# A decoder layer with routed experts on one core: token rows scattered to the experts, results scattered back by token

## What is computed

```python
x = _layernorm(x + _L0_attn_ref(x, ...))      # a mamba block: in-projection, conv, selective scan, out-projection
x = _layernorm(x + _L0_xattn_ref(x, ctx, ctx, ...))  # attention to the context, layer norms, FFN 256 -> 1024 -> 256
x = _layernorm(x + _L0_ffn_ref(x, ...))       # the experts, below
# experts: a router gives each token 8 of 160 experts, with gates that sum to 2.5
#   routed = sum over the token's 8 experts of  gate * (silu(x @ w_gate[e].T) @ w_down[e].T)   (256 -> 128 -> 256)
#   shared = silu(x @ w_gate_shared.T) @ w_down_shared.T
#   result = routed + shared
```

## Time and profile before

| | |
|---|---|
| runs | 1699.87 us median (1698.13 to 1703.37) |
| the profiled execution's own time | 1708.86 us |
| its span | 1707.1 us |
| PE, DVE, ACT, POOL busy | 1000.4, 1122.7, 580.4, 880.6 us |
| DVE in 40 slices (tenths) | 1898989999999899999998423344434322224444 |
| POOL in 40 slices | 1545355555655565466374643554544445455664 |
| DMA in 40 slices | 7322140500501401302300000577767787633332 |
| TensorE's granted clock, mean | 0.795 of full speed |

### The profile page before, as it was taken

How to read it: one execution, slowest core, us unless ns; L and a number is a source line. 1 busy time by engine, 2 the same in 40 slices (tenths; PEclk the granted TensorE clock), 3 DMA queues, 4 the chain that set the end, 5 groups by cost and what they waited for, 6 DMA issues and landing times. The chain is left out here.

```text
span 1707.1 us, 20590 instructions
## 1 busy us (share of the span) xinstructions
PE 1000.4 (59%) x4460; PEld 801.9 (47%) x4460; DVE 1122.7 (66%) x2190; ACT 580.4 (34%) x1476; POOL 880.6 (52%) x751
## 2 busy tenths in 40 slices
PE   4567778586676676676577650477767676710000
PEld 2445567474565565564465540466656555500000
DVE  1898989999999899999998423344434322224444
ACT  3564647346335345344342110133332333300000
POOL 1545355555655565466374643554544445455664
PEclk8788789698798788787888775698889899955555
DMA  7322140500501401302300000577767787633332
GB/s 237 128 72 102 44 142 15 183 1 20 179 2 49 149 13 51 135 13 62 117 13 19 13 6 7 160 204 215 209 197 218 195 240 213 188 120 102 106 115 80
DMA packets 118558, 185.00 MB, mean 108 GB/s; under 512 B 16225, under 2 KB 82529, under 8 KB 118114
## 3 DMA queue, kind: packets, MB, share of 16 engines
q1 hardware_dynamic: 97426, 137.72, 24.4%
q0 software_dynamic: 21072, 46.64, 11.2%
HBM read 152.26 MB, written 57.22 MB: 123 GB/s over the span
## 5 line engine op out<-in xcount | busy, mean ns | idle before, releaser
L413 POOL TENSOR_TENSOR inf<-bc,du 128x1024 f32<-128x1024 f32 x128 | 302.0, 2365 | 194.0 <-DVE DA L974 85.0
L743 PE MATMUL Y<-hb,ident 128*128 128x256 f32 x1024 | 280.2, 423 | 60.7 <-DVE hb L981 37.4
L1335 POOL DMA_INDIRECT xg<-x_dram,idb x216 | 205.6, 952 | 207.3 <-DVE idb L1493 94.3
L974 DVE TENSOR_TENSOR_SCAN DA<-DA,inf 128x1024 f32<-128x1024 f32 x128 | 292.8, 2287 | 8.2 <-ACT DA L593 5.9
L743 PEld LDWEIGHTS Y<-hb,ident 128*128 128x128 f32 x1024 | 216.1, 216 | 110.9 <-DVE hb L981 46.3
L593 ACT ACTIVATE DA<-dl,a_neg 128x255 f32<-128x255 f32 x512 | 211.7, 460 | 0.2
L1376 PE MATMUL DA<-wt,h 128*128 128x256 f32 x432 | 148.7, 430 | 66.9 <-ACT h L1402 57.2
L1369 PE MATMUL DA<-xgT,wt 128*128 128x128 f32 x864 | 152.4, 304 | 49.2 <-DVE xgT L1490 26.5
L1607 POOL DMA_INDIRECT G<-y_dram,si x128 | 122.4, 957 | 88.6 <-issue 38.2
L466 POOL DMA_INDIRECT tok_dram<-id_st,ad_i x128 | 131.9, 1030 | 67.1 <-issue 34.0
L981 DVE TENSOR_TENSOR hb<-DA,bc 128x1024 f32<-128x1024 f32 x128 | 156.4, 1222 | 9.8
(11 more groups left out here) (219 smaller groups left out, 1782.2 us busy)
## 6 DMA issues: line engine op xcount, KB each, us to landing
wt<-in_w_moe SPq DMA_DIRECT2D x216, 256.0 KB
bc<-bc_dram SPq DMA_DIRECT2D x32, 1024.0 KB, 5.3
y_dram<-ys SPq DMA_DIRECT2D x54, 512.0 KB
y_dram<-zeros SPq DMA_DIRECT2D x8, 2560.0 KB, 9.9
xg<-x_dram,idb POOLq DMA_INDIRECT x216
xt<-in_xT SPq DMA_DIRECT2D x8, 256.0 KB, 5.2
w<-in_w SPq DMA_DIRECT2D x2, 1024.0 KB, 6.8
ct<-in_cT SPq DMA_DIRECT2D x8, 256.0 KB, 3.3
```

The source lines that it names most:

```text
L413: g.tensor_tensor(inf[t % NI][:, :, :], bc[gr][:, 0, :, :], du[p][:, c, :].unsqueeze(1).to_broadcast([P, SG, T]), ALU.mult).then_inc(inflo ...
L743: ins = mm(Y[:, 0:T], ident[:, :], hb[t % NH][:, n, :], start=gr == 0 and n == 0, stop=gr == NG - 1 and n == SG - 1, skip_group_check=True)
L974: v.tensor_tensor_scan(da[:, :], da[:, :], inf[t % NI][:, :, :].rearrange("p n t -> p (n t)"), 0.0, ALU.mult, ALU.add).then_inc(scan_d.sem, 1)
L1335: g.indirect_dma_start(xg[s_][:, :], None, x2_dram, bass.IndirectOffsetOnAxis(ap=idb[s_][:, 0:1], axis=0)).then_inc(xg_in[s_].sem, 16)
```

## The change

**Front.** The row of a token becomes 273 words (`XW`): 256 of x2, 8 expert numbers, 8 gates, and the token's number times 8. x2 lives in two such buffers `x2e`. The 16 indirect DMAs per batch scatter these whole rows (1092 B) to `xe_dram`, at expert x 1536 + rank; the 16 ranks are no longer read one by one: the table of counts plus `home` (expert x 1536) is multiplied by the mask of chosen experts, and the eight largest values are the addresses. Rows past 1536 of an expert would go to `xo_dram`; that can happen only in batches 6 and 7 (`crowded`), which get three more DVE instructions and 16 more scatters each; with these inputs all of these are out of bounds and write nothing. The first 128 rows of each expert in both arrays are zeroed from ACT's queue. `x2_store`, `y_clear`, the zeroing of `tok_dram` and ACT's copy of the counts go.

**Experts.** A block's tokens lie together, so SP loads them by a direct DMA (`tokens`), followed by one from `xo_dram` (`tokens_over`) and by the weights; each has its own table entry and condition. DVE finds for each row which of its 8 experts this is (`look_up`), and from it the gate and the row in `yp_dram`; ACT applies the gate as it copies the result, and POOL scatters each block's 128 rows, token-major.

**Combine.** A tile's 8 rows per token lie together. SP loads 1 MB per tile, DVE adds one half to the other, PE sums the four quarters and the accumulator by products with the identity, and DVE normalises.

```diff
-            def rank(b, choices):
-                for c in choices:
...
-                    v.scalar_tensor_tensor(junk[k % 2][:, :], iota_e[:, :], e_st[:, q, k:k + 1], cum[:, q, :],
-                                           ALU.is_equal, ALU.mult, accum_out=r_st[:, q, k:k + 1]).then_inc(rank_s.sem, 1)
+            def lanes(b):
+                dve.wait_ge(cum_f.sem, cum_f.at(b, 1))
...
+                v.tensor_tensor(cum[:, :, :], QF[:, 0:QT * NE].rearrange("p (q e) -> p q e", q=QT),
+                                home[:, :].unsqueeze(1).to_broadcast([P, QT, NE]), ALU.add).then_inc(cum_c.sem, 1)
             def address(b):
...
+                v.scalar_tensor_tensor(rep[:, :, :], rep[:, :, :], 0.0, cum[:, :, :], ALU.is_gt, ALU.mult).then_inc(addr.sem, 1)
...
+                for q in range(QT):
+                    v.max(ad_f[:, q, :], rep[:, q, :]).then_inc(addr.sem, 1)
...
-                g.indirect_dma_start(tok_dram, bass.IndirectOffsetOnAxis(ap=ad_i[:, q, k:k + 1], axis=0),
-                                     id_st[:, q:q + 1], None).then_inc(scat.sem, 16)
+                g.indirect_dma_start(xe_dram, bass.IndirectOffsetOnAxis(ap=ad_i[:, q, k:k + 1], axis=0),
+                                     x2e[p][:, q, :].bitcast(I32), None, bounds_check=LIM - 1, oob_is_err=False).then_inc(scat.sem, 16)
...
-            SCATTER_AT = (4, 4, 5, 5, 5, 6, 7, 8, 9, 9, 11, 12, 12, 13, 13, 13)
+            SCATTER_AT = (3, 3, 4, 4, 5, 5, 6, 7, 8, 9, 9, 11, 12, 13, 13, 13)
...
-                        if t == 15:
+                        if t == 15 and not (isinstance(s, int) and s - 3 == NB - 1):
+                            if crowded(s - 3):
+                                for c in range(QT * TOPK):
+                                    scatter_over(s - 3, 1 - p, c)
                             settle(s - 3)
...
+            def clear_near(n):
+                lo, hi = n * NE // 3, (n + 1) * NE // 3
+                rows_ = xe_dram.rearrange("(e r) w -> r e w", e=NE)[0:P, lo:hi, :]
+                s.dma_start(rows_, zeros[:, :].bitcast(I32).unsqueeze(1).to_broadcast([P, hi - lo, XW])).then_inc(blank.sem, 16)
...
+                    if t == 4 and isinstance(s, int) and 0 <= s < 3:
+                        clear_near(s)
+                    elif t == 4 and exists(s) and not (isinstance(s, int) and s < 0):
+                        clear_rest(s)
...
-            sp.dma_start(tab[0:1, :], blk_dram.rearrange("f j -> (f j)").unsqueeze(0)).then_inc(tab_in.sem, 16)
+            sp.dma_start(tab[:, :], blk_dram.rearrange("f j -> (f j)").unsqueeze(0).broadcast_to([P, 6 * NBLK])).then_inc(tab_in.sem, 16)
...
+            def tokens(i, s_):
+                j = column[s_] + i
+                w = nc.values_load(tab[0:1, bass.ds(j + 2 * NBLK, 1)], engines=[mybir.EngineType.SP], min_val=0, max_val=4 * LIM,
...
+                if xgT_f.at(i - 1, s_ + 1, True):
+                    sp.wait_ge(xgT_f.sem, xgT_f.at(i - 1, s_ + 1))
+                    sp.wait_ge(pid_d.sem, pid_d.at(i - 1, s_ + 1))
                 sp.sem_inc(tick, 1)
+                sp.dma_start(xg_i[s_][:, :], xe_dram[bass.ds(r, P), :], cond=w < LIM).then_inc(xg_in[s_].sem, 16)
+            def tokens_over(i, s_):
+                j = column[s_] + i
+                w = nc.values_load(tab[0:1, bass.ds(j + 3 * NBLK, 1)], engines=[mybir.EngineType.SP], min_val=0, max_val=NE * REST,
...
+                sp.dma_start(xg_i[s_][:, :], xo_dram[bass.ds(r, P), :], cond=w < NE * REST).then_inc(xg_in[s_].sem, 16)
+            def body(i):
                 for s_ in range(UNROLL):
+                    tokens(i, s_)
+                    tokens_over(i, s_)
                     weights(i, s_)
-                    if s_ % YG == YG - 1:
-                        store(i - 1, s_ // YG)
             for s_ in range(UNROLL):
+                tokens(0, s_)
                 first_weights(s_)
+            sp.wait_ge(scat_o.sem, 2 * 16 * QT * TOPK)
+            for s_ in range(UNROLL):
+                tokens_over(0, s_)
...
+            for c in range(QT * TOPK):
+                q, k = c // TOPK, c % TOPK
+                g.indirect_dma_start(xo_dram, bass.IndirectOffsetOnAxis(ap=ad_o[:, q, k:k + 1], axis=0),
...
+            def scatter(i, s_):
+                pool.wait_ge(pid_d.sem, pid_d.at(i, s_ + 1))
+                pool.wait_ge(dn_c.sem, dn_c.at(i, s_ + 1))
...
+                g.indirect_dma_start(yp_dram, bass.IndirectOffsetOnAxis(ap=pid[s_][:, 0:1], axis=0), ys[s_][:, :], None,
...
+            def weighted(i, s_):
+                act.wait_ge(gt_d.sem, gt_d.at(i, s_ + 1))
...
+                s.activation(ys[s_][:, :], DN[s_ % 2][:, 0:D], ACT.Identity, scale=gt[s_][:, 0:1]).then_inc(dn_c.sem, 1)
...
+            def look_up(i, s_):
+                e = tab_e[:, bass.ds(last * s_ + (i + s_), 1)]
+                dve.wait_ge(xg_in[s_].sem, xg_in[s_].at(i, 32))
+                if dn_c.at(i - 1, s_ + 1, True):
+                    dve.wait_ge(dn_c.sem, dn_c.at(i - 1, s_ + 1))
+                    dve.wait_ge(y_sc[s_].sem, y_sc[s_].at(i - 1, 16))
...
+            def load(t):
...
+                sp.dma_start(Y8[i][:, :], yp_dram[t * P * TOPK:(t + 1) * P * TOPK, :].rearrange("(p k) d -> p (k d)", p=P)).then_inc(y_in[i].sem, 16)
+                sp.dma_start(ac[i][:, :], acc_dram[t * P:(t + 1) * P, :]).then_inc(y_in[i].sem, 16)
...
+                for k in range(TOPK // 2):
+                    nc.tensor.matmul(bank[:, 0:D], ident[:, :], Y8[i][:, k * D:(k + 1) * D], start=k == 0, stop=False)
+                nc.tensor.matmul(bank[:, 0:D], ident[:, :], ac[i][:, :], start=False, stop=True).then_inc(sum_f.sem, 1)
```

More of the change, by code:

```diff
@@ L225, in decoder_kernel @@
         x2a = sf("x2a", [P, QT, D])
-        x2 = sf("x2", [P, QT, D])
+        x2 = [x2e[i][:, :, 0:D] for i in range(2)]
         hs = sf("hs", [P, T])
@@ L1297, in weights @@
                 sp.dma_start(wt[s_][:, :], a["w_moe"][bass.ds(e * P, P), :], cond=w < NE).then_inc(wt_in[s_].sem, 16)
-            def store(i, h):
-                sp.wait_ge(dn_c.sem, dn_c.at(i, (h + 1) * YG))
-                sp.sem_inc(tick, 1)
-                rows_ = y_dram[bass.ds((i * UNROLL + h * YG) * P, YG * P), :]
-                sp.dma_start(rows_.rearrange("(j p) d -> p j d", p=P), ys[h][:, :, :]).then_inc(y_st[h].sem, 16)
-            def body(i, sure):
+            def tokens(i, s_):
+                j = column[s_] + i
+                w = nc.values_load(tab[0:1, bass.ds(j + 2 * NBLK, 1)], engines=[mybir.EngineType.SP], min_val=0, max_val=4 * LIM,
+                                   skip_runtime_bounds_check_because="the table holds rows of xe_dram, and more than their number")
+                r = nc.s_assert_within(w, 0, LIM - P, skip_runtime_bounds_check_because="the copy is left out from LIM on")
+                if xgT_f.at(i - 1, s_ + 1, True):
+                    sp.wait_ge(xgT_f.sem, xgT_f.at(i - 1, s_ + 1))
+                    sp.wait_ge(pid_d.sem, pid_d.at(i - 1, s_ + 1))
+                sp.sem_inc(tick, 1)
+                sp.dma_start(xg_i[s_][:, :], xe_dram[bass.ds(r, P), :], cond=w < LIM).then_inc(xg_in[s_].sem, 16)
@@ new lines, in tokens_over @@
+            def tokens_over(i, s_):
+                j = column[s_] + i
+                w = nc.values_load(tab[0:1, bass.ds(j + 3 * NBLK, 1)], engines=[mybir.EngineType.SP], min_val=0, max_val=NE * REST,
+                                   skip_runtime_bounds_check_because="the table holds rows of xo_dram, or their number")
+                r = nc.s_assert_within(w, 0, NE * REST - P, skip_runtime_bounds_check_because="the copy is left out for their number")
+                sp.dma_start(xg_i[s_][:, :], xo_dram[bass.ds(r, P), :], cond=w < NE * REST).then_inc(xg_in[s_].sem, 16)
@@ L1313, in _ @@
             further_turns(sp, last, body)
-            for h in range(UNROLL // YG):
-                store(last, h)
-            for h in range(UNROLL // YG):
-                sp.wait_ge(y_st[h].sem, y_st[h].at(last, 16))
-                sp.sem_inc(tick, 1)
         @block.gpsimd
@@ L1463, in _ @@
+            for c in range(3):
+                ins = v.scalar_tensor_tensor(junk2[0:BJ, 9 + c, :], incl[0:BJ, :], jn[:, c:c + 1], one_f[0:BJ, :], ALU.is_le, ALU.mult,
                                              accum_out=blk_p[:, c:c + 1])
             link(ins)
+            v.scalar_tensor_tensor(blk_b[:, :], over[:, :], -float(NEAR // P), blk_b[:, :], ALU.mult, ALU.add)
+            link(v.scalar_tensor_tensor(blk_n[:, :], over[:, :], -float(NEAR), blk_n[:, :], ALU.mult, ALU.add))
+            link(v.tensor_scalar(blk_q[:, :], blk_n[:, :], float(NEAR), -float(P), ALU.min, ALU.add))
@@ L1556, in decoder_kernel, with body @@
+            def body(i):
+                for s_ in range(UNROLL):
+                    turned(i, s_)
+                    look_up(i, s_)
+            body(0)
+            further_turns(dve, last, body)
+        mid.close()
+        y_in = [sig(f"y_in{i}", 32) for i in range(NY)]
```

(21 more changed lines are left out.)

545 lines of the change are left out of this document (239 added, 306 removed).

## The result

The changed kernel takes 1822.8 us in the median of four runs (1820.1 to 1825.2), the kernel before 1699.0 (1693.5 to 1703.4): a ratio of 1.073, between 1.070 and 1.077. The forecast was 1949 with a range of 1835 to 2075. The sign, the stage and the mechanism are as forecast; the size is not, and the time lies 12 us outside the range. Nearly all of the error is in one term, the price of a block on SP's queue in the expert stage.

The account below looks back on a forecast made before the run. SP's own look-up instructions were taken to bound the expert stage; -26 + 0 + 8.5 + 19 + 368 + 10 - 129 = +250.5 turned span 1707.1 into 1957.6, own time 1959.4, median 1949 us; range 1835 to 2075.

Parts of the forecast that it names:

- table and first turn: Before the expert loop: wider table, longer DVE chain, 16 more SP copies issued or skipped; +19 us, bounds +10 and +30.
- expert loop: Expert stage: three looked-up copies per block on SP, 3.76 us x 208 blocks = 782 against 413.6; +368 us.
- end of the stage: Expert stage's end: last block's load, two products, scatter and its landing follow instead of one store; +10 us, +4 to +15.
- combine: Combine stage: 128 gathers replaced by 16 large tiles at 4.0 us of PE each, 74 us against 203.3; -129 us.
- What bounds the kernel: Expert stage: SP's queue, occupied by its own look-up instructions and hardly waiting, sets the pace at 1.99 us per block.
- 3.36 us of SP per block: Expert loop, SP without stall: tokens 1.31, skipped overflow copy 0.82, weights 1.17, loop branch 0.06.
- I take 0.4 per block: Expert loop: SP's stall beside POOL's single scatters, 0.4 us per block, below the 0.5 before; ends 0 and 1.0.
- The second rival: Expert loop: every scatter stops SP for 1.0 us, 4.36 per block, +125 us, total 2073; chance 0.10.
- The fourth rival: Expert loop: part of the look-up is saved, 2.55 to 3.2 us per block, total 1700 to 1835; chance 0.07.
- Front: 300 to 800 us: 16 narrow DVE instructions per batch go, about six replace them; -26 us, between -35 and -10.
- third rival: Front: clears and scatters push bc loads late in DVE-bound turns, +60 us, total 2009; chance 0.07.
- Drain: After the front: 16 out-of-bounds scatters of batch 6 on POOL delay batch 7's addresses; +8.5 us, between 0 and +12.

Follow-up runs that it names:

- The burst run: Changed kernel with POOL waiting for four weighted blocks, then issuing four scatters back to back: 1931.9 us against 1822.8; repeated at 1929.1 and 1942.3.
- the kernel with 16 operations back: Changed kernel with 16 operations of the removed 128x160 form per batch back on VectorE, results unread: 1837.7 us in set 2, 1837.2 in set 4.
- set 4: Runs on one chip: kernel before 1709.4 us (1712.4 as base), changed kernel 1823.3, scatters in bursts of four 1942.3, 16 operations back 1837.2.
- set 2: Runs on another chip, where the kernel before took 1593.9 us; 16 operations back took 1837.7; the unedited changed kernel has no run there.
- the folded value: Changed kernel with overflow look-ups only in turns needing one, told by one value per turn that VectorE folds and SP loads: 1709.1 us, ratio to before 1.005.

## Why the prediction missed

Term by term, in us of span:

| term | foreseen | measured |
|---|---|---|
| front and drain | -17.5 | -26.3 |
| table and first turn | +19 | +17.4 |
| expert loop | +368 | +245.7 |
| end of the stage | +10 | +15.6 |
| combine | -129 | -138.3 |
| sum | +250.5 | +114.1 |

**What bounds the kernel**: right. SP's queue bounded the stage before (a look-up more costs 109 us) and bounds it now (taking look-ups away gives 114 and 192).

**Expert loop**: the step that failed. I put 3.76 us on a block; it is 3.17, and 0.59 by 208 is 122 of the 136 us of error. Two parts of it were mis-sized. The smaller is the price of the look-ups without a stall, "3.36 us of SP per block": about 3.07. The token copy (1.31) and the skipped one (0.82) were right within 0.1, but I took three in four weight copies as fetched, "160 of 216 blocks at least taken". Only 112 or 113 of the loop's 208 are (by the length of the issue), so "at least" was wrong; the others keep the expert of the block before them in their buffer. That makes 1.17 into 1.04. The larger is "I take 0.4 per block" for the stall: it is about 0.1. I had written in the sentence before it that the scatters would come singly, and had the earlier trace rows for what four copies cost away from packed gathers, and still carried over four fifths of the old stall. The burst run, with nothing but the grouping changed, shows both ends of this term: 0.1 with single scatters, 0.5 more with packed ones. Even the 0.1 is not all stall: the kernel with 16 operations back, whose loop is the same, takes 3.17 per block in set 4 and 3.15 on the chip of set 2, where SP isn't stopped. The second rival (1.0 us for every scatter) is refuted by the same run: the burst's first scatter cost nothing. The fourth rival's time came true, 1700 to 1835, by another mechanism than it named: no part of the look-up is saved. "Overflow, always skipped here" was wrong by one copy.

**Front**: the turns got shorter by 6.7 us (122.1 to 115.4), not 4.2, and with 37.5 us at the last MAX8 the term lies outside its own bounds (-35 and -10). The 16 operations put back account for 3.5 us of it; the rest is open but for the 2.1 us named above. The larger clears and scatters cost nothing that shows: third rival out. **Drain**: right in kind. +8.5 was foreseen for the 16 scatters ahead of the last batch; from the last MAX8 to the end of the barrier it is 48.4 us for 37.2, +11.2, within the bounds of 0 and +12, and moving the scatters makes it 35.9.

**Table and first turn**: right within 2 us in the sum, with two steps that err against each other: from the barrier to SP's first copy +5.3 us (3.5 foreseen), from there to the loop about +12 (17 foreseen). The eight overflow look-ups took 5.95 us there.

**End of the stage**: 18.5 us from SP's last copy to the combine's first load. The last scatter starts at 1744.64; behind it a DRAIN of 9.04 us stands on POOL before the barrier, which I had not counted.

**Combine**: 9 us under the forecast, and by another bound. I had PE set the pace, at 4.0 us per tile; the transfers do, at 3.4 per tile. From 1760 to 1800:

```profile
1760.00:1800.00 40.00, 29.02 (x111) 22.26 (x112) 27.30 (x61) 2.03 (x10) 0.00 (x0) 0.90 0.99 382
```

PE had the full clock there soon (granted clock 0.80 from 1760 to 1780, 1.00 from 1780 on): a tile's products take 1.99 and 0.59 us, 2.6 in all, under the 3.4 from tile to tile. I had taken 4.0 on the ground that PE leaves a stage in which it is seldom busy. That the term came out within 9 us is luck, since a tile was priced by the wrong bound; what came true is the low end given for it, 64 us with everything hidden in the DMA.

**The range**: its lower end stood at 3.25 us per block, and for the number of weight copies, which had no row behind it, it had no lower bound. With half of them fetched and no stall a block is 3.23; with the front and the combine at the low ends that the text itself gave them (9 and 10 us), it would have begun at 1949 - 110 - 19 = 1820 and held the result.

## What to carry to other kernels

Count the instructions that a queue executes for each run-time addressed copy, taken or not, and put that sum beside the engines' busy times: here 0.8 to 0.95 us for a skipped copy and 1.2 for a taken one cost 246 us where the combine gained 138, and moving one of the three look-ups to a queue with room turned +7% into -4%. A stall that comes from two engines' coincidence is not a constant: work it out from the spacing that the new kernel will have. Where it is large it can swallow part of what an edit adds (0.51 of 0.8 us added in the kernel before). And when an edit pays less than expected, look first at what the edit itself put in: of the 0.74 us per block that the folded value saved, 0.14 went to its own load and branches. Work taken from ahead of a barrier may only move: 9 us gained at the barrier were 4 at SP's overflow look-ups on one chip, and 11 gained there were 1 on another. When kernels with and without such coincidences are compared, one chip is not enough.

## What I had not expected of the hardware

POOL's indirect DMAs stop SP's instruction stream for about 0.7 us each when they are issued 1.28 us apart (109 us for 162 scatters in bursts), and by under 0.1 us in the mean in the changed kernel, where the one before is mostly over 2 us back. Three chips show it and a fourth does not; with the same program the longest record of one weight copy is 0.71 us on one and 0.35 us on the other. Why SP stops was not shown. A skipped look-up costs SP all but 0.25 us of a taken one. A scatter with hardly a row in bounds takes POOL the same 1.28 us as one that writes 128 rows.
